# Global values of a block-sparse attention in column halves, their row sums from the exponential, and the order of finish, maximum and top-k on VectorE

## The reference, cut to what matters

```
q, k, v = heads of (layernorm(x) @ W + b)
ctx = local attention: query block of 128 tokens against 256 keys around it
idx = [0] + top 62 tokens by |q| of this head + [1023]        # 64 queries
g_ctx = softmax(q[idx] @ k.T / sqrt(32)) @ v                  # against all 1024 keys
ctx[idx] = g_ctx
x = x + layernorm(ctx); then the experts on layernorm(x)
```

## Time and profile before

| | |
|---|---|
| Median of 3 runs | 905.24 us |
| Profiled execution, its own time | 906.39 us |
| Its span | 904.6 us |
| PE busy | 820.6 us, 91% |
| DVE, ACT, POOL busy | 574.1 (63%), 402.3 (44%), 139.3 us (15%) |
| Mean granted TensorE clock | 0.963 |
| Chain that ended last | PE 71%, DVE 16%, DMA 5%, issue 3%, ACT 3% |

### The profile page before, as it was taken

One profiled execution on the slowest core, in us unless ns is written; L12 is line 12 of the kernel. 1 busy time (PEld: TensorE's weight loads), 2 busy tenths in 40 slices (PEclk: granted clock), 3 DMA queues, 4 the chain that ended last, 5 costly groups with the idle time before them and its releaser, 6 DMA issues.

```text
span 904.6 us, 13737 instructions
## 1 busy us (share of the span) xinstructions
PE 820.6 (91%) x5060; PEld 673.2 (74%) x5060; DVE 574.1 (63%) x1230; ACT 402.3 (44%) x771; POOL 139.3 (15%) x199
## 2 busy tenths in 40 slices
PE   2999999988979799899789989979999999999994
PEld 2676867776858578677567778779999999887783
DVE  5544996347878355666348854436667677648565
ACT  2423242315555365555644333346666667633120
POOL 4000002220000400121113652100000000012222
PEclk9999999989999799999979889989999999999998
DMA  6697545973675566772216862256777777745544
GB/s 205 185 297 223 171 136 180 261 228 103 186 215 145 137 185 173 200 198 85 65 43 215 273 221 87 68 188 211 218 229 217 216 224 222 222 142 161 175 129 139
DMA packets 117442, 162.38 MB, mean 179 GB/s; under 512 B 17316, under 2 KB 65188, under 8 KB 117376
## 3 DMA queue, kind: packets, MB, share of 16 engines
q1 hardware_dynamic: 113792, 153.54, 56.0%
q0 software_dynamic: 3584, 7.97, 3.1%
HBM read 107.24 MB, written 55.05 MB: 179 GB/s over the span
## 4 chain that ended last, share of the span: by engine, by line
PE 71%; DVE 16%; DMA 5%; issue 3%; ACT 3%; POOL 1%; SPq 0%; DVEq 0%; POOLq 0%; another core or an unknown queue 0%; ACTq 0%
PE bank L163 44%; PE wide L163 20%; PE wide L167 4%; PE bank L167 3%; DVE SG L160 2%; DMA scr_v<-vt 2%; DMA H<-scr_oe,FG 2%; DVE STC L273 1%; DMA scr_xd<-H,FSI 1%; DVE MX L160 1%; DVE CX L1381 1%; DVE SIL L149 1%; DVE XT L149 1%; DVE CT L149 1%; DVE TI L647 1%
## 5 line engine op out<-in xcount | busy, mean ns | idle before, releaser
L163 PE MATMUL bank<-XT,W13H 128*128 128x256 f32 (+1 forms) x1056 | 243.4, 326 | 3.1 <-DVE XT L149 3.1
L163 PEld LDWEIGHTS bank<-XT,W13H 128*128 128x128 f32 x1056 | 176.3, 191 | 19.4 <-ACT W13H L145 1.9
L163 PE MATMUL bank<-XT,W13L 128*128 128x256 f32 (+1 forms) x528 | 170.1, 322 | 0.0
L163 PE MATMUL wide<-W2H,HH 128*128 128x512 f32 x352 | 117.5, 400 | 3.8 <-DVE CX L1381 3.6
L160 DVE TENSOR_REDUCE MX<-wide 128x1 f32<-128x192 f32 (+1 forms) x128 | 77.2, 649 | 62.7 <-PE wide L163 52.2
L163 PEld LDWEIGHTS bank<-XT,W13L 128*128 128x128 f32 x528 | 100.9, 191 | 8.3
L149 DVE TENSOR_TENSOR SIL<-bank,SIL 128x256 f32<-128x256 f32 (+1 forms) x72 | 36.9, 512 | 74.9 <-ACT SIL L157 74.3
L157 ACT ACTIVATE PT<-bank 128x512 f32<-128x512 f32 x128 | 72.4, 594 | 24.7 <-PE bank L163 21.6
L163 PEld LDWEIGHTS wide<-W2H,HH 128*128 128x128 f32 x352 | 67.6, 192 | 19.8 <-DVE CX L1381 5.3
L157 ACT ACTIVATE SIL<-bank 128x256 f32<-128x256 f32 (+1 forms) x72 | 32.7, 454 | 110.1 <-PE bank L163 109.1
L163 PE MATMUL wide<-W2L,HH 128*128 128x512 f32 x192 | 76.3, 397 | 0.0
(11 more groups left out here) (201 smaller groups left out, 1507.3 us busy)
## 6 DMA issues: line engine op xcount, KB each, us to landing
R<-in_L_ffn_W_dram SPq DMA_DIRECT2D x48, 512.0 KB, 5.3
scr_q<-hl SPq DMA_DIRECT2D x16, 512.0 KB, 4.2
scr_k<-hl SPq DMA_DIRECT2D x16, 512.0 KB, 3.8
R<-in_L_ffn_sw_dram SPq DMA_DIRECT2D x12, 512.0 KB, 5.3
QSe<-scr_q SPq DMA_DIRECT2D x36, 128.0 KB, 3.1
KSe<-scr_k SPq DMA_DIRECT2D x36, 128.0 KB, 3.3
scr_v<-vt SPq DMA_DIRECT2D x16, 272.0 KB, 2.4
R<-_attn_hidden_states_dram SPq DMA_DIRECT2D x16, 256.0 KB, 3.9
```

The lines of the kernel that those rows point to most:

```text
L163: return do("pe", lambda g: g.matmul(ps, a, b, start=start, stop=stop, skip_group_check=True), after, mark=mark)
```

## The change

Columns: the value tile now holds one head pair in 68 columns, one of ones, 64 values, three of ones. Local values take 33 of them from either side (sum first for even heads, last for odd). Global values take only the 64 values; even tiles go to PSUM partitions 0 to 63, odd ones to 64 to 127, all nine in one group in step 0 of the next pair. The row sums come from the exponential (`accum_out`), and the finish adds the two halves. In the order: `local_finish` stands right behind `local_turn`, back and finish of the last pair behind it in step 1, and the global maximum behind both. The top-k of batch 1 is cut in 23 single steps at k = 3, 5, 6, 7 of the first six pairs, `topk_ids` moves to g = 48, `rows_1` to 50. Tiles of stage 1 that are stored from (`vt`, `hl`, `qt`) are allocated first and so lie under the late head buffers and CT only; the other tiles of stage 2, GT and `stack_q` wait for `fence_ps` alone.

```diff
-VW = HD + 2
+VW = 2 * HD + 4
...
+            vtr = Ring([sb(st, f"vt{i}", [P, HEADS // 2, VW]) for i in range(2)], [slot(), slot()])
+            hl = Ring([sb(st, f"hl{i}", [P, 2, 512], F32R) for i in range(4)], [slot() for _ in range(4)])
+            qtr = Ring([sb(st, f"qt{i}", [P, 512]) for i in range(2)], [slot(), slot()])
...
             for b in vtr.bufs:
-                m_vone = do("pool", lambda g, b=b: g.memset(b[:, :, HD:VW], 1.0))
+                do("pool", lambda g, b=b: g.memset(b[:, :, 0:1], 1.0))
+                m_vone = do("pool", lambda g, b=b: g.memset(b[:, :, 2 * HD + 1:VW], 1.0))
...
-            def topk_round(b, r):
+            def topk_part(b, r, part):
...
+                if part == 0:
+                    m = do("dve", lambda g: g.max(v8, N_[:, :]), prev)
+                elif part == 1:
+                    m = do("dve", lambda g: g.max_index(i8, v8, N_[:, :]), prev)
+                else:
+                    m = do("dve", lambda g: g.match_replace(N_[:, :], v8, N_[:, :], -1.0), prev)
+                tk[b]["m"] = m
...
+            CT = ring("CT", 2, [P, NB, P], slots=True, first=fence)
...
-            OS = ring("OS", 2, [OB + VW, 512])
-            PG = ring("PG", 1, [P, SEQ], first=fence)
-            SG = ring("SG", 2, [P, 4], first=fence)
+            OS = ring("OS", 2, [P, 512])
+            PG = ring("PG", 1, [P, SEQ])
+            SG = ring("SG", 2, [P, 4])
...
-                    m_zgt.append(do("pool", lambda g: g.memset(f(GT[:, :, 64:128]), 0.0), begun + [a3]))
+                    m_zgt.append(do("pool", lambda g: g.memset(f(GT[:, :, 64:128]), 0.0), fence_ps + [a3]))
...
-                             stacked[b] + wfree + begun, mark=(k == 7))
+                             stacked[b] + wfree, mark=(k == 7))
...
-                v0 = (n % 4) * VW
+                v0 = (n % 4) // 2 * VW + (HD + 1) * (n % 2)
...
-                m_x = red(sg[:, 0:1], wb[:, :], ALU.max, [m_s] + sgfree)
-                m_b = ts(sg[:, 1:2], sg[:, 0:1], -SCALE, None, ALU.mult, None, [m_x])
...
             def global_exp(i):
                 g_ = gp[i]
+                sg = g_["sg"]
+                m_x = red(sg[:, 0:1], g_["w"][:, :], ALU.max, [g_["m_s"]] + g_["sgfree"])
+                g_["m_b"] = ts(sg[:, 1:2], sg[:, 0:1], -SCALE, None, ALU.mult, None, [m_x])
                 g_["m_e"] = act(g_["pg"][:, :], g_["w"][:, :], ACT.Exp, [g_["m_b"]] + g_["pgfree"],
-                                bias=g_["sg"][:, 1:2], scale=SCALE)
+                                bias=g_["sg"][:, 1:2], scale=SCALE, accum_out=g_["sg"][:, 3:4])
...
+            def global_values(i):
...
+                v0 = (i % 2) * VW + 1
+                g_["wi"], w, wfree = W_.take()
+                for r in range(3):
+                    pi, pt, m_c = g_["pt", r]
+                    for k, t in enumerate(TILES[r]):
+                        row = 64 * (t % 2)
+                        m_o = mm(w[row:row + 64, 0:P], V["v"][:, t, v0:v0 + 2 * HD], pt[:, k * P:(k + 1) * P], t < 2, t > 6,
+                                 [m_c, V["m"], m_vzero[V["i"]]] + wfree, mark=(k == len(TILES[r]) - 1))
...
-                m_c = copy("act", os[0:2 * VW, 0:P], w[0:2 * VW, 0:P], [m_o] + sfree)
+                m_c = copy("act", os[:, 0:P], w[:, 0:P], [m_o] + sfree)
...
-                g_["m_t"] = tr(tb[:, 0:2 * VW], os[0:2 * VW, 0:P], ident[0:2 * VW, 0:2 * VW], [m_c, m_id] + tfree, mark=True)
+                g_["m_t"] = tr(tb[:, 0:P], os[:, 0:P], ident[:, :], [m_c, m_id] + tfree, mark=True)
...
+                m_r = do("dve", lambda g: g.reciprocal(sg[:, 2:3], sg[:, 3:4]), [g_["m_e"]])
+                halves = []
                 for s in range(2):
                     rw = slice(64 * s, 64 * s + 64)
...
+                    c0 = HD * s
+                    m_c = copy("dve", GC[rw, i, :], w[rw, c0:c0 + HD], [g_["m_t"]])
+                    halves.append(tt(GC[rw, i, :], GC[rw, i, :], w[rw, 64 + c0:64 + c0 + HD], ALU.add, [m_c]))
+                m_f = ts(GC[:, i, :], GC[:, i, :], sg[:, 2:3], None, ALU.mult, None, [m_r] + halves)
...
-            chores = {1: late_rows, 46: lambda: topk_ids(1), 48: rows_1, 56: lambda: stack_split(1),
+            chores = {1: late_rows, 48: lambda: topk_ids(1), 50: rows_1, 56: lambda: stack_split(1),
                       63: lambda: stack_q(1)}
-            for r in range(8):
-                chores[6 * r + 3] = lambda r=r: topk_round(1, r)
+            parts = [(r, part) for r in range(8) for part in range(3) if r < 7 or part < 2]
+            for at, (r, part) in zip([g for g in range(48) if g % 8 in (3, 5, 6, 7)], parts):
+                chores[at] = lambda r=r, part=part: topk_part(1, r, part)
...
                 if g >= 5 and g % 4 == 1:
                     local_turn((g - 5) // 4)
+                    local_finish((g - 5) // 4)
+                if k == 1 and i > 0:
+                    global_back(i - 1)
+                    global_finish(i - 1)
+                if k == 1 + late and i < 16:
+                    global_exp(i)
                 if g >= 4 and g % 4 == 0:
                     for u in range(4):
                         local_values(g // 4 - 1, u)
                 if k == 4 and i < 15:
                     row_shift(2 * i + 2, ST_)
                     row_max(2 * i + 2 + ROW_MAX[k][0], ROW_MAX[k][1])
...
+                if i < 16 and 4 <= k - late < 7:
+                    global_turn(i, k - 4 - late)
+                if k == 0 and i > 0:
+                    global_values(i - 1)
```

More of the change, by code:

```diff
@@ L111, in sandwich @@
     kd = nc.dram_tensor("scr_k", (2, D, T), F32, kind="Internal").ap()
-    vd = nc.dram_tensor("scr_v", (T, HEADS * VW), F32, kind="Internal").ap()
+    vd = nc.dram_tensor("scr_v", (T, HEADS // 2 * VW), F32, kind="Internal").ap()
     qtok = nc.dram_tensor("scr_qtok", (T, D), F32, kind="Internal").ap()
@@ L639, in sandwich, with topk_round @@
             tk = [{} for _ in range(2)]
-            def topk_round(b, r):
+            def topk_part(b, r, part):
                 N_, V_, I_ = NRM[b], TV[b], TI[b]
-                prev = [tk[b]["m"]] if r else list(m_nrm[2 * b:2 * b + 2])
+                prev = [tk[b]["m"]] if r + part else list(m_nrm[2 * b:2 * b + 2])
                 v8 = V_[:, 8 * r:8 * r + 8]
                 i8 = I_[:, 8 * r:8 * r + 8]
[L646 to L650, removed]
+                if part == 0:
[5 more added lines that the diff above has]
+                tk[b]["m"] = m
+            def topk_round(b, r):
+                for part in range(3 if r < 7 else 2):
+                    topk_part(b, r, part)
             def topk_step(u):
@@ L928, in global_turn @@
                 g_["pt", r] = (pi, pt, m_c)
-            def global_values(i, r):
+            def global_values(i):
                 g_ = gp[i]
                 V = vq[i // 2]
[L934 to L945, removed]
+                v0 = (i % 2) * VW + 1
[6 more added lines that the diff above has]
+                                 [m_c, V["m"], m_vzero[V["i"]]] + wfree, mark=(k == len(TILES[r]) - 1))
+                    PTG.busy[pi].append(m_o)
                 if i % 2 == 1:
@@ L964, in global_finish @@
                 ti, w = g_["back"]
+                m_r = do("dve", lambda g: g.reciprocal(sg[:, 2:3], sg[:, 3:4]), [g_["m_e"]])
+                halves = []
                 for s in range(2):
                     rw = slice(64 * s, 64 * s + 64)
[L967 to L970 removed]
+                    c0 = HD * s
+                    m_c = copy("dve", GC[rw, i, :], w[rw, c0:c0 + HD], [g_["m_t"]])
+                    halves.append(tt(GC[rw, i, :], GC[rw, i, :], w[rw, 64 + c0:64 + c0 + HD], ALU.add, [m_c]))
+                m_f = ts(GC[:, i, :], GC[:, i, :], sg[:, 2:3], None, ALU.mult, None, [m_r] + halves)
                 SG.busy[g_["sgi"]].append(m_f)
[L972 removed]
+                ST_.busy[ti].append(halves[1])
                 g_["m_f"] = m_f
@@ L1033, in slot_of @@
                     row_max(2 * i + 2 + ROW_MAX[k][0], ROW_MAX[k][1])
-                for p in (i - 1, i):
-                    if 0 <= p < 16:
-                        at = g - 8 * p - (1 if p == 0 else 0)
-                        if 4 <= at < 7:
-                            global_turn(p, at - 4)
-                        if 5 <= at < 8:
-                            global_values(p, at - 5)
-                        if at == 8:
-                            global_back(p)
-                            global_finish(p)
-                if k == 1 + late and i < 16:
-                    global_exp(i)
-                if g >= 5 and g % 4 == 1:
-                    local_finish((g - 5) // 4)
+                if i < 16 and 4 <= k - late < 7:
+                    global_turn(i, k - 4 - late)
+                if k == 0 and i > 0:
+                    global_values(i - 1)
                 if k == 4 and i % 2 == 0 and 0 < i < 16:
```

28 lines of the change are left out of this document (10 added, 18 removed).

## The result

The changed kernel takes 941.08 us (median of 4 runs, 937.44 to 941.36), the kernel before 904.20 us in the same job (4 runs, 902.50 to 905.47). The ratio is 1.040, 95% interval [1.0367, 1.0433]: slower by 37 us. The profiled run is the fastest of the four, 937.44 us with a span of 935.7, so 31.0 us above the profiled 906.4 of before (31.1 between the spans). The forecast was 928, its range 896 to 948.

The account below looks back on a forecast made before the run. Taken as bound by each pair's chain through maximum and exponentials, with TensorE 91% busy. Terms -3.5 + 2.6 + 2.3 + 11.8 + 2.7 + 2.4 + 4.5 = +22.8 on 906.4: 929.2, median 928 us; range 896 to 948.

Parts of the forecast that it names:

- The chain: Per pair, finishes ahead of the maximum delay PG to 3.9 us after global scores end (T); pairs 7-14 +11.8 us.
- The clock: Half clock on TensorE after the some 3 us gap in each pair: three events, +4.5 us, bounds 0 to 15.
- rival of half clock after nearly every pair's gap: Across the pairs, 12 more half-clock events at 1.5 us each, kernel at 946 us; chance 0.14.
- the end: After pair 15's last local values, global values and global_finish follow, the chain costs 2.1 us; +2.7 us in all.
- Pairs 0 to 5: Pairs with the top-k in single steps, bound by VectorE's work at 16.5 us each; +2.6 us, bounds -6 to +8.
- Global values: 18 records on column halves in 1.05 us a pair instead of 1.98; 1.05 of 1.98 recovered in steps 5 to 7.
- Row sums: In ScalarE's exponentials, the sum costs 0.15 us a pair on the path, bounds 0 to 0.27; +2.4 us.
- The start: Attention start: transposes no longer wait for scr_v's store, pair 0's global scores end at 198.5, not 202.05; -3.5 us.
- Pair 6: The pair beside the gathers, 24.3 us before: +2.3 us; its stop of all engines may shift some 6 us.
- PE-bound: Whole kernel: the maximum's delay costs nothing and TensorE's saved work counts in full; 887 us, chance 0.20.
- The mild case: Steps 5 to 7 give back all 1.98 us, sums are free, no half clock; 912 us, chance 0.14.
- The case in which gains and losses cancel: Whole kernel: gains at the start and in top-k gaps cancel the chain's losses; 905 us, chance 0.05.

Follow-up runs that it names:

- e3: Changed kernel plus nine extra 512-column matmuls, result overwritten, ahead of the local values of step 4 in each pair but the first: 927.26 us, ratio 1.0236.
- e2: Kernel before with only the order changed: local_finish behind local_turn, last pair's back and finish in step 1, global maximum behind both: 933.11 us, ratio 1.0284.
- e7: Changed kernel with the exponential PG issued in step 3 instead of step 1, VectorE's order as changed: 900.99 us, ratio 0.9947.
- e4: Kernel before with only the start edits: stage 1 stored tiles allocated first, CT ahead of PT, fence_ps at GS, GT, PG, SG: 903.12 us, ratio 0.9978.
- e5: Changed kernel with maximum right behind global scores, back and finish in step 0, column-half values spread over steps 5 to 7: 902.21 us, ratio 0.9964.
- e6: e5 with local finish ahead of the global maximum and the exponential PG in step 3: 892.57 us, ratio 0.9867.
- e10: Kernel before with e4's start, top-k in single steps, local finish ahead of the maximum, PG in step 3: 891.31 us, ratio 0.9837.
- e12: e7 with the turn back and global finish of the pair before moved from step 1 to step 3: 897.09 us, ratio 0.9906.
- e13: e12 with the top-k's single steps in steps 0, 3, 5, 6 instead of 3, 5, 6, 7: 883.99 us, ratio 0.9898.

## Why the prediction was right, and where it was off

**The chain, right.** The forecast had PG at T + 3.9, the transpose at T + 6.6, a pair of 15.9 us; measured were T + 3.61 and T + 6.85 with half clock, and T + 6.40 and 15.98 us in e3 without it. What was said to be late next is what the waits name: ACT PT, 30.6 us over 16 times. e2 shows that the order alone does it, e7 that the queue behind PG carries it. The six operations took 1.17 us and not 1.4.

**The clock, mis-sized.** This is the term that failed: +4.5 us for three events. The windows show half clock in nearly every pair; e3 sizes it at 1.4 us each, 18.3 us over thirteen pairs and 14.7 in all. That is the rival of half clock after nearly every pair's gap, with its price about right (1.5) and its chance too low (0.14). I let one row in which full clock followed a wait of 2.95 us outweigh two in which it did not. With 14.7 in place of 4.5 the sum is 22.8 + 10.2 = 33.0 us on the profiled run, with 18.3 it is 36.6, where 31.0 were measured; the end, 5.4 us below its forecast, works the other way. That the forecast's 929.2 for this run lay only 8.2 us off is thus in part luck. The Trainium skill (TensorE: Matmul & The Clock Gate, "HAM oscillation") speaks of repeated idle gaps in a loop that put the clock back each time; here the trace agrees, pair after pair, though the gaps told of there are longer waits for DMA and those of pair 12 are 0.51 and 1.89 us. That such gaps recur is not enough by itself: with 0.51 and 0.43 us in e7 the clock stayed at 0.99.

**Pairs 0 to 5, right in size but not in the reason.** In e3 the middle ones are 16.2 to 16.3 us (forecast 16.5), and most of the rest of the +9.8 is the clock. But the forecast had them bound by DVE's work, with the global scores waiting for the wide buffer of step 0's maximum. In the kernel after that wait is 0.6 us in all, in three places, and the one on ACT PT is 9.5 us over pairs 1 to 5: they go by the same chain as the later pairs, and the size came out right by luck. The working's own sum is also 0.3 us lower than it says: 14.0 + 5 x 16.5 less a step of 1.28 is 95.2, not 95.5.

**Global values, pace right, place half right.** 18 records in 1.26 us, of which about 1.19 pass before the next scores, for 1.05 forecast. The way from the transpose behind the values to the next T took 9.57 us in e3 (405.41 + 1.09 - 396.93), for 9.3: steps 5 to 7 gave back less than the 1.05 us assumed.

**Row sums, smaller.** The exponential keeps its 1.11 us and a separate operation of 0.19 us follows; the next exponential starts 1.11 us after PG's start where it was 1.01. That is 0.10 us a pair, 1.6 in all, for 2.4.

**The start, right in place and not in worth.** T of pair 0 was forecast at 198.5 and came at 198.50. e4 shows that alone it doesn't shorten the whole by an amount that can be measured.

**Pair 6 and the end.** Pair 6 lost 4.6 us for 2.3. It holds the stop beside the gathers, and it took 17.6 to 29.4 us in the kernels here; which part of it is the change's wasn't separated. Behind T of pair 15 the profiled run is 2.7 us shorter, for +2.7 longer. The same stretch was 466 to 471 us long in these kernels, which share the code behind the attention; a part of that size can't be put down to the change.

**The rivals.** PE-bound (887) fell: PG at T + 3.61 is past its point of T + 2.5. e7 shows what it missed: the 0.93 us that PE saves is not what a pair is bound by, and where the chain is removed, the waits on DVE (GC, MX) come next. The mild case (912) fell on all three of its conditions: steps 5 to 7 did not give back all 1.98 us, the sums were not free, and the clock halved. The case in which gains and losses cancel (905) fell with the pairs 7 to 14, which alone lost 23.0 us.

## What to carry to other kernels

In a queue that is worked in order, ask of each late instruction what stands behind it: PG was equally late in the kernel after (941 us) and in e7 (901 us), and only what was queued behind it differed. A wait of TensorE that comes back in each round may have to be priced with the half clock behind it: here 1.4 us on waits of 0.5 and 1.9 us, and nothing on waits of 0.5 and 0.4 us (e7). A rare event in the trace of before says little on a wait that becomes regular. For column halves, count the changes of mode, 0.17 us each, against the columns saved: spread in three groups they saved nothing (e5, e6 against e10), and that one group makes the kernel faster is not shown either (e12).

## What the runs showed of the hardware

- An exponential with a row sum is followed by ACTIVATION_READ_ACCUMULATOR, 0.19 us, which delays the next by 0.10 us.
- Going into and out of column halves costs 0.17 us each; eight records take 0.66 us where they took 1.04.
- Work whose result is thrown away made a kernel 14 us faster, by keeping TensorE at 2.4 GHz through a wait.
- A single wait of 1.06 us was followed by half clock in e13, while one of 2.95 us in the kernel before was not the earlier trace rows. Waits of 0.51 and 0.43 us in each pair of e7 left the clock at 0.99. What decides is not settled by these runs.
